# State-space mixer on one core: the decay difference clamped in eight VectorE instructions, the causal mask folded into B times C

## The reference, cut to what matters

```
A_dt = (dt * A) in chunks;  A_cum = cumsum(A_dt, axis=-1)      # falls along the chunk, A < 0
diff[l, s] = A_cum[l] - A_cum[s];  mask = tril(ones(c, c))     # l >= s
L = exp(where(mask, diff, -inf))
Y_diag = einsum('bzlhn,bzshn,bhzls,bzshp->bzlhp', Cc, Bc, L, xch)
...
decay_states = exp(A_cum[..., -1:] - A_cum)
states = einsum('bzlhn,bhzl,bzlhp->bzhpn', Bc, decay_states, xch)
```

## Time and profile before

| | before |
|---|---|
| median of 3 runs | 1849.84 us (1848.43 to 1850.89) |
| span of the profiled execution | 1849.7 us |
| PE matmul busy | 1693.5 us, 92% |
| DVE busy | 1464.4 us, 79% |
| ACT busy | 1186.5 us, 64% |
| POOL busy | 1362.0 us, 74% |
| POOL's mask L1245, 128 times | 182.4 us busy |
| DVE's difference L1115, 128 times | 202.5 us busy |

### The profile page before, as it was taken

One profiled execution on the slowest core, in us unless ns is written; L12 is line 12 of the kernel. 1 busy time (PEld: TensorE's weight loads), 2 busy tenths in 40 slices (PEclk: granted clock), 3 DMA queues, 4 the chain that ended last, 5 costly groups with the idle time before them and its releaser, 6 DMA issues.

```text
span 1849.7 us, 32321 instructions
## 1 busy us (share of the span) xinstructions
PE 1693.5 (92%) x9616; PEld 1372.8 (74%) x9616; DVE 1464.4 (79%) x2214; ACT 1186.5 (64%) x1627; POOL 1362.0 (74%) x933
## 2 busy tenths in 40 slices
PE   7789999899998989989899999989999898998989
PEld 4568778687777867777687777867777786777867
DVE  7695986959789595977959689695977959598695
ACT  5674865747667574866658577574856758477562
POOL 1494985949679494985949689494976949588594
PEclk9899999999999999999999999999999999999999
DMA  5542432423344242433434344342433334243231
GB/s 205 198 134 79 159 117 101 132 78 136 107 131 137 83 128 82 154 113 102 136 110 152 102 131 138 94 118 95 140 113 113 123 100 128 89 151 117 94 103 46
DMA packets 121876, 220.40 MB, mean 119 GB/s; under 512 B 30176, under 2 KB 46560, under 8 KB 121312
## 3 DMA queue, kind: packets, MB, share of 16 engines
q1 hardware_dynamic: 121824, 219.76, 37.1%
HBM read 212.88 MB, written 6.82 MB: 119 GB/s over the span
## 4 chain that ended last, share of the span: by engine, by line
POOL 43%; PE 32%; issue 19%; DVE 2%; ACT 1%; POOLq 0%; DVEq 0%; ACTq 0%
POOL w_low L1219 11%; POOL square_sum L1225 8%; POOL scores L1245 8%; POOL xdecay L1264 8%; POOL y L1231 7%; PE bank L770 6%; PE bank L772 6%; PE bank L771 6%; POOL out_low L1254 3%; PE bank L732 3%; PE bank L733 2%; PE bank L734 2%; PE bank L809 1%; PE bank L869 1%; DVE scores L1115 1%
## 5 line engine op out<-in xcount | busy, mean ns | idle before, releaser
L1219 POOL TENSOR_TENSOR w_low<-raw,w_high 128x512 fp32r<-128x512 f32 x285 | 399.6, 1402 | 390.2 <-DVE scores L1115 312.7
L732 PE MATMUL bank<-x_high,w_high 128*128 128x512 f32 x1140 | 484.5, 425 | 6.3 <-POOL w_low L1219 4.1
L733 PE MATMUL bank<-x_low,w_high 128*128 128x512 f32 x1140 | 457.1, 401 | 0.0
L734 PE MATMUL bank<-x_high,w_low 128*128 128x512 f32 x1140 | 455.5, 400 | 0.0
L1019 DVE SCALAR_TENSOR_TENSOR hs<-bank,cols,hs 128x511 f32<-128x511 f32 x381 | 280.7, 737 | 40.1 <-ACT hs L896 40.0
L732 PEld LDWEIGHTS bank<-x_high,w_high 128*128 128x128 f32 x1140 | 219.8, 193 | 73.6 <-issue 31.5
L734 PEld LDWEIGHTS bank<-x_high,w_low 128*128 128x128 f32 x1140 | 218.6, 192 | 53.4
L733 PEld LDWEIGHTS bank<-x_low,w_high 128*128 128x128 f32 x1140 | 220.6, 193 | 41.7
L1033 DVE TENSOR_TENSOR scores<-scores,bc 128x1024 f32<-128x1024 f32 x128 | 242.1, 1891 | 3.7 <-ACT bc L994 3.7
L1264 POOL TENSOR_TENSOR xdecay<-xdt,tables 128x384 f32<-128x384 f32 x128 | 215.7, 1685 | 37.1 <-DVE xdt L1150 37.1
L905 ACT ACTIVATE w_high<-raw 128x512 fp32r<-128x512 f32 x285 | 177.2, 622 | 97.8 <-PE bank L734 90.9
(11 more groups left out here) (135 smaller groups left out, 2933.2 us busy)
## 6 DMA issues: line engine op xcount, KB each, us to landing
raw<-w_in SPq DMA_DIRECT2D x288, 256.0 KB, 2.7
sums<-sums_dram SPq DMA_DIRECT2D x128, 512.0 KB, 3.7
out_raw<-w_out SPq DMA_DIRECT2D x128, 256.0 KB, 3.6
grown_rows<-grown_dram SPq DMA_DIRECT2D x256, 96.0 KB, 3.4
xt<-x SPq DMA_DIRECT2D x8, 256.0 KB, 5.0
mixed<-x SPq DMA_DIRECT2D x2, 1024.0 KB, 7.6
table_dram<-table SPq DMA_DIRECT2D x2, 768.0 KB, 3.7
tables<-table_dram SPq DMA_DIRECT2D x32, 48.0 KB, 2.1
```

Of the source, the lines that this page charges most:

```text
L732: pe.matmul(to[:], w_high[:, slot, k], x_high[:, b, k], start=(k == 0), stop=False)
L733: pe.matmul(to[:], w_high[:, slot, k], x_low[:, b, k], start=False, stop=False)
L734: mm = pe.matmul(to[:], w_low[:, slot, k], x_high[:, b, k], start=False, stop=(k == KT - 1))
L1219: pool.tensor_tensor(w_low[:, t % SPLIT], raw[:, t % RAW], w_high[:, t % SPLIT].bitcast(F32), ALU.subtract).then_inc(w_low_ready, 1)
```

## The change

DVE's difference is cut into eight instructions, one for each of two heads and four chunks (128 elements a partition each). Each subtracts a column and takes the minimum with zero, so the exponential of a masked place is at most 1. ACT's exponential waits for the last of the eight. POOL's mask and its wait are gone. A 128x128 matrix `causal` of ones and zeros is made once by POOL at the start, and at each boundary DVE multiplies B times C by it on the way from `turn_bank` to `bc`, where ACT's copy was.

```diff
-                        s.wait_ge(masked, step * UNITS + q + 1)
+                        s.wait_ge(diff_ready, step * UNITS + q + 1)
                         s.activation(scores[:, q % 2], scores[:, q % 2], ACT.Exp).then_inc(exp_ready, 1)
...
-                if nxt is not None:
-                    s.wait_ge(bc_product, nxt[0] + 1)
-                    s.activation(bc[:].rearrange("p c l -> p (c l)"), turn_bank[:], ACT.Copy).then_inc(bc_ready, 1)
...
-                        col = table_of(SUMS, q).rearrange("p r c -> p (r c)")
-                        v.tensor_tensor(scores[:, q % 2].rearrange("p r c l -> p (r c) l"),
-                                        sums[:, q % 2].rearrange("p r c l -> p (r c) l"),
-                                        col.unsqueeze(2).to_broadcast([P, PAIR * CHUNKS, P]), ALU.subtract)\
-                         .then_inc(diff_ready, 1)
+                        col = table_of(SUMS, q)
+                        for r in range(PAIR):
+                            for c in range(CHUNKS):
+                                op = v.tensor_scalar(scores[:, q % 2, r, c], sums[:, q % 2, r, c], col[:, r, c:c + 1],
+                                                     0.0, ALU.subtract, ALU.min)
+                        op.then_inc(diff_ready, 1)
...
                 if nxt is not None:
+                    v.wait_ge(bc_product, nxt[0] + 1)
+                    v.tensor_tensor(bc[:], turn_bank[:].rearrange("p (c l) -> p c l", c=CHUNKS),
+                                    causal[:].unsqueeze(1).to_broadcast([P, CHUNKS, P]), ALU.mult)\
+                     .then_inc(bc_ready, 1)
                     v.wait_ge(bc_ready, nxt[0] + 1)
                     score(nxt[0], 0)
...
-                    if ahead:
-
-                        pool.wait_ge(diff_ready, ahead[0] * UNITS + ahead[2] + 1)
                     for step, g, t in splits[:1]:
                         low_part(step, t)
-                    if ahead:
-
-                        at = scores[:, ahead[2] % 2].rearrange("p r c l -> p (r c) l")
-                        pool.affine_select(out=at, in_=at, compare_op=ALU.is_ge, fill=MASKED, base=0,
-                                           pattern=[[0, PAIR * CHUNKS], [1, P]], channel_multiplier=-1)\
-                            .then_inc(masked, 1)
```

More of the change, by code:

```diff
@@ L52 @@
 TABLE_STORES = 16 * 4
-MASKED = -1e30
 def reached(eng, semaphore, value):
@@ L100, in build @@
         mixed = sb("mixed", [P, CHUNKS, HID])
-        ident = sb("ident", [P, P])
+        ident, causal = sb("ident", [P, P]), sb("causal", [P, P])
         mean_col = sb("mean_col", [P, 2])
@@ L114, in build, with prologue @@
                                         "conv_ready"))
-        prologue(nc, bank, x_high, x_low, mixed, ident, mean_col, eps_col, buffers, loads, counts, x_tokens, w_dt,
+        prologue(nc, bank, x_high, x_low, mixed, ident, causal, mean_col, eps_col, buffers, loads, counts, x_tokens, w_dt,
                  dt_bias, a_log, w_dense, lora_a, lora_b, probs, w_in, conv_bc, unit_cols, dense_dram,
                  sums_dram, grown_dram, table_dram, chunk_dram)
-        mixer(nc, bank, x_high, x_low, mixed, ident, mean_col, eps_col, buffers, loads, counts, x_tokens, w_in,
+        mixer(nc, bank, x_high, x_low, mixed, ident, causal, mean_col, eps_col, buffers, loads, counts, x_tokens, w_in,
               conv_bc, unit_cols, w_out, bias, dense_dram, sums_dram, grown_dram, table_dram, chunk_dram,
               mixed_dram, out_tokens)
-def prologue(nc, bank, x_high, x_low, mixed, ident, mean_col, eps_col, buffers, loads, counts, x_tokens, w_dt, dt_bias,
+def prologue(nc, bank, x_high, x_low, mixed, ident, causal, mean_col, eps_col, buffers, loads, counts, x_tokens, w_dt, dt_bias,
              a_log, w_dense, lora_a, lora_b, probs, w_in, conv_bc, unit_cols, dense_dram, sums_dram, grown_dram,
@@ L161, in prologue @@
         small_in, lora_in, wd_in, mixed_in = sem("small_in"), sem("lora_in"), sem("wd_in"), sem("mixed_in")
-        ident_ready = sem("ident_ready")
+        ident_ready, causal_ready = sem("ident_ready"), sem("causal_ready")
         stats_ready, moments_ready, std_ready, rstd_ready, xn_ready, turned, high_ready, low_ready = (
@@ L223, in _ @@
             pool.memset(ident[:], 0.0).then_inc(ident_ready, 1)
+            pool.memset(causal[:], 1.0).then_inc(ident_ready, 1)
             pool.memset(mean_col[:], 1.0 / (INTER // GROUPS)).then_inc(ident_ready, 1)
@@ L226, in _ @@
             pool.memset(ones[:], 1.0).then_inc(ident_ready, 1)
-            pool.wait_ge(ident_ready, 1)
+            pool.wait_ge(ident_ready, 2)
             pool.affine_select(out=ident[:], in_=ident[:], compare_op=ALU.not_equal, fill=1.0, base=0,
                                pattern=[[-1, P]], channel_multiplier=1).then_inc(ident_ready, 1)
+            pool.affine_select(out=causal[:], in_=causal[:], compare_op=ALU.is_ge, fill=0.0, base=0,
+                               pattern=[[1, P]], channel_multiplier=-1).then_inc(causal_ready, 1)
             for t in range(SPLIT):
@@ L236, in _ @@
         def _(pe):
-            pe.wait_ge(ident_ready, 5)
+            pe.wait_ge(ident_ready, 6)
             def turn_x(tb):
@@ L329, in inverse_of @@
                 s.activation(inverse[:, b], logged[:, b], ACT.Exp, scale=-1.0).then_inc(inverse_ready, 1)
-            s.wait_ge(ident_ready, 5)
+            s.wait_ge(ident_ready, 6)
             s.activation(warm[:], eps_col[:], ACT.Sqrt)
@@ L516, in _, with mixer @@
                 table_of(i)
-def mixer(nc, bank, x_high, x_low, mixed, ident, mean_col, eps_col, buffers, loads, counts, x_tokens, w_in, conv_bc,
+            v.wait_ge(causal_ready, 1)
+def mixer(nc, bank, x_high, x_low, mixed, ident, causal, mean_col, eps_col, buffers, loads, counts, x_tokens, w_in, conv_bc,
           unit_cols, w_out, bias, dense_dram, sums_dram, grown_dram, table_dram, chunk_dram, mixed_dram,
@@ L566, in mixer @@
         mixed_store, mixed_load = sem("mixed_store"), sem("mixed_load")
-        (gate_ready, hs_ready, turned, xdt_ready, xdecay_ready, diff_ready, masked, exp_ready, scores_ready,
+        (gate_ready, hs_ready, turned, xdt_ready, xdecay_ready, diff_ready, exp_ready, scores_ready,
          diag_done, states_added, state_link, state_ready, carried, skip_added, carry_scaled, y_sum, y_ready,
@@ L571, in mixer @@
             sem(n) for n in ("gate_ready", "hs_ready", "turned", "xdt_ready", "xdecay_ready", "diff_ready",
-                             "masked", "exp_ready", "scores_ready", "diag_done", "states_added", "state_link",
+                             "exp_ready", "scores_ready", "diag_done", "states_added", "state_link",
                              "state_ready", "carried", "skip_added", "carry_scaled", "y_sum", "y_ready",
```

## The result

The changed kernel takes 1877.87 us (median of 4 runs, 1876.16 to 1878.90) against 1849.61 (1848.43 to 1850.89): a ratio of 1.0148, 95% interval 1.0134 to 1.0163. It is **1.5% slower**, where 1837 us was forecast. The trace's span grew by 24.7 us, from 1849.7 to 1874.4.

What follows compares the result with a forecast made beforehand. DVE and POOL taking turns at SBUF were taken to bound mid-step units, PE the boundary. Gains of 4 x 0.10 + 0.4 = 0.8 us a step, 13 in 16 steps, gave 1837 us from 1849.7; range 1785 to 1890.

Steps and rivals of the forecast that it cites:

- The turns of one engine at a time: Mid-step: DVE and POOL alternate on two-input SBUF data, so a unit sums their turns; 10.72 us after the change, 0.10 less.
- the 0.19 us between small ones: DVE's eight 128-element differences: 0.19 us from start to start, 0.27 each, 1.60 for all when unblocked.
- POOL getting in at the second and third: Mid-step: waiting POOL runs between the eight, so their second and third take about 1.1 and 1.4 us.
- the squares behind the product: Mid-step: DVE's product of scores is ready 0.10 us ahead of POOL's squares and goes first.
- POOL's idle time ahead of the gate: Mid-step: POOL idles about 2 us before the gate on y while DVE makes five small differences, `grown_rows` and `y`.
- The boundary: Between steps: DVE's added `causal` product, 0.68 us, is covered by 2.41 us of DVE idle time, so costs nothing.
- Rivals 1 and 2: Eight differences: 1, DVE keeps its turn throughout, 1792 us, chance 0.13; 2, they exclude nobody, 1714 us, chance 0.06.
- rival 3: Mid-step: POOL's squares get in ahead of DVE's product of scores, unit 0.7 us longer, 1900 us; chance 0.13.
- rival 4: Each small difference costs more, 0.25 us apart with turns taken, no gain at the step's start, 1866 us; chance 0.22.
- The start of a step: Units 0 to 3: POOL has slack, and unit 3's `xdecay` comes about 0.4 us earlier; bounds nothing and 1.0.
- PE bounds nothing: Mid-step: `xdecay` keeps its place 1.95 us behind the product, so PE's wait stays near 1.9 us.

Runs made afterwards that it cites:

- experiment 3: Kernel before, with B times C multiplied by `causal` on DVE at the boundary instead of copied by ACT, single difference and POOL's mask kept: 1850.53 us, ratio 1.0000.
- experiment 4: Kernel before, with the difference in eight tensor_scalars and POOL's mask kept: 1934.74 us, ratio 1.0464.
- experiment 7: Changed kernel, with one subtraction on DVE and the clamp on ACT (Relu of the negative, then exponential of its negative): 1761.50 us, ratio 0.9518.
- Experiment 1: Changed kernel, with 120 one-column memsets added at the end of DVE's prologue to shift its instruction list: 1860.68 us, ratio 1.0061.

## Why the prediction was wrong

**Right.** The turns of one engine at a time, the 0.19 us between small ones, POOL getting in at the second and third, the squares behind the product, POOL's idle time ahead of the gate: 10.70 us where 10.72 was forecast, against 10.83. The boundary: 37.22 against 37.29, and experiment 3 shows the `causal` product free. Rivals 1 and 2 fell by the 3.73 us of the eight; rival 3 because the squares end behind the product; rival 4 because the spacing was the 0.19 taken.

**Wrong, first: "The start of a step".** It walked unit 2 alone, up to `xdecay`, and gave 0.4 us of gain. Counted from tap to tap, the first two cycles lose 1.00 and 0.69. That step failed twice: the eight in unit 1, ahead of it, were never costed (3.30 us for 1.22, with 0.93 of idle time as the only cover), and `xdecay` was the wrong end to walk to, since it is made ahead of the eight. So also "PE bounds nothing": PE's wait did not stay with `xdecay`, it went to `state`. Per step: 1.69 - 5 x 0.13 - 0.07 = +0.97, and 109.85 becomes 110.82, where -0.8 was forecast.

**Wrong, second: what isn't in the sum.** DVE's 57 more instructions in a loop body were costed as work only, not as code. The stalls took 19.0 us in steps 9 to 14. No row of before hints at them, for there DVE has no such wait; but the Trainium skill's section named above did speak against the change and should have stood among the rivals, with the count of instructions.

**A gain that the prediction had no term for.** In the windows view of before, two boundaries from tap to tap (start and end, length, busy us of PE, PEld, DVE, ACT and POOL, granted clock, DMA share, GB/s):

```profile
1032.91:1071.74 38.83, 38.83 (x187) 32.09 (x185) 16.78 (x29) 15.26 (x23) 13.83 (x12) 0.96 0.20 59
1144.29:1181.58 37.29, 37.29 (x183) 31.10 (x185) 16.57 (x29) 15.26 (x23) 13.87 (x12) 1.00 0.19 60
```

The longer has a piece at the lower clock, 0.96 on the mean, and costs 1.54 us. Counting a step from its own first tap to that of the next, six of steps 1 to 14 have such a piece in their boundary before and none after: -9.2 us. What PE did ahead of such a piece is in the last section.

The sum over the traces closes, with steps counted in this way: -1.3 up to DVE's first tap of `bc_conv` in step 0, +2.3 from there to the first tap of step 1, 14 steps of +0.97 make +13.6, stalls +19.0, clock -9.2, last step and what follows it +0.2: +24.6 of the 24.7 us seen.

## What to carry to other kernels

Where two engines take turns at SBUF, an instruction cut in eight gives its turn away as often as the other engine has something ready; what it costs is paid back only in units where DVE was held up before, so walk the first units of a step as well as the middle one, and as far as the last instruction that another engine waits for. Count the instructions that an edit adds to a hardware loop, and look for idle time put down to `issue` at its start: it can move or vanish with padding ahead of the loop. A causal mask on POOL ahead of an exponential can become a clamp on ACT if ACT has room: here, with ACT 64% busy before, it took 4.8% off the whole kernel.

## What the runs showed of the hardware that was not expected

A waiting POOL gets in between two DVE instructions whose starts are only 0.19 us apart (in mid-step the first of the eight, held by the squares, took 0.72 us, the second 0.88, the third 1.31, the last five 0.28 each).

The mean granted clock is 0.974 in before, 0.972 in experiment 3 and 0.969 in experiment 4, all with POOL's mask, and 0.994 to 0.997 in the kernels without it; behind the prologue the trace of before shows 25 dips of 3.4 us to the lower of the two levels (1.2 of 2.4 GHz), and the changed kernel 3. PE is busy for 89 to 94% in all of them, so its busy share does not sort them (92% before, 94% in experiment 7). What sorts the kernels is how long PE waits within the units. In before, 24 of the 25 dips begin within 1.6 us of the end of a wait of 1.95 to 1.98 us for `xdecay`; in experiment 4, 31 of 33 do so behind waits of 2.06 to 2.17 us, for `state`. The changed kernel's usual wait is 1.56 us and no dip follows one; its three dips follow waits of 1.90 to 2.11 us in the units behind a stall. Experiment 1 is the same kernel without the stalls, and from step 1 on it has no dip. So the gain in clock goes with PE's shorter wait, not with the mask as such. That the wait causes the dip is argued and not shown: most waits of 1.97 us are followed by none, and no run changed them alone.
